# Threshold search of a mixture-of-experts router: one of three counts on ScalarE, mantissa digits in float sums

## The chip, the cores and the metric

The kernel runs on one core of a Trainium2 chip. The metric is the device time of one execution in microseconds. Engines are named as in the profile: PE is TensorE, DVE is VectorE, ACT is ScalarE, POOL is GpSimd, SP issues loads and stores.

## What is computed

One transformer block on x of shape (2, 2048, 256): a modulated layer norm, linear attention with 16 heads, then a second modulated layer norm and a mixture of 8 experts with 2 experts for each token and a capacity of 640 tokens for each expert. The change lies in how the tokens of an expert are picked. Cut to that part, the reference is:

```python
probs = jax.nn.softmax(xf @ router_w.T, axis=-1)          # (4096, 8)
topw, topi = jax.lax.top_k(probs, 2)
topw = topw / (topw.sum(-1, keepdims=True) + 1e-06)
order = jnp.lexsort((-fw, fe))                            # by expert, then by weight, falling
rank = jnp.arange(N * K) - starts[se]
keep = rank < capacity                                    # 640 largest weights of each expert
...
eo = jnp.einsum('ecf,efd->ecd', jax.nn.silu(g) * u, wd)
out = jnp.zeros_like(xf).at[st].add(gathered * (sw * keep)[:, None])
```

So each expert needs the 640 largest of its weights. The kernel does not sort: it finds, for each of the 8 experts at once, the largest threshold that at least 640 weights reach, and takes what lies above it.

## The kernel before, in words

Each engine has a program written out by hand; semaphores order them. There are three stages.

*Attention*, one tile of 128 tokens after the other (32 tiles), as a software pipeline over steps (`step` in each engine's program). POOL's last work in it is, for each tile, `xm` (L479) and `h2` (L483). ACT copies each tile's router logits into `logits` (L603) and signals `lgc`.

*Routing.* `choose` on DVE (L773 to L792) turns logits into the two weights of each token, once for the first 26 tiles and once for the last 6; ACT supplies the exponentials (`exp_logits`, L546). PE transposes the weights (L1292), so that 128 partitions hold 256 weights each, 16 partitions to an expert. Then comes the search: `cand` holds three thresholds as integers whose bits are those of positive floats. The loop over `DIGITS` = 15 base-4 digits, from the top of the exponent down, does one round for each:

- DVE counts in each partition how many weights reach each of the three thresholds (L895, three times, each with a sum as second output in `cnt`),
- PE adds the counts of the partitions of an expert (`same_e`, L1296),
- DVE prepares `base` meanwhile (L899), then compares the three sums with 640 (`beats`, L901), takes the largest digit that passes (`won`, L904) and writes the next three thresholds (`cand`, L906). Each of the three waits for the one before.

The tables `digits` and `swaps` for it are set by POOL at the start, one memset for each element (L442, L443). After the loop the threshold goes to all partitions (L909, PE L1298, L911), masks and counts give each token its slot in the expert, `describe(0)` makes one-hot rows by comparing with `iota_b` (L975), and PE looks up the token numbers with them (L1317). Their result `g_idx` (L989) starts POOL's gathers (L500). `iota_b`, 4096 columns of row numbers, is written by ACT behind the last exponential (L622), and behind it ACT makes the high parts `w_h` of the first six blocks of expert 0's weights (L629), whose low parts DVE makes after the search. `reset` (L494, L496) is set by POOL once all logits are there and is read behind the search.

*Experts.* For each of 8 experts PE runs gate, up and down projections in three passes with high and low parts (L1354, L1368); ACT and DVE work on the hidden values beside it. The expert stage begins once the first gathers have landed.

Of the kernel before, what the change touches and what calls it, by code (L numbers as in the profile page):

```python
# [26 lines left out]
N = B * T  # L27
NT = N // P
# [4 lines left out]
CAP = int(1.25 * N / E)  # L33
# [3 lines left out]
FC = F // P  # L37
# [7 lines left out]
TOP_BIT = 29  # L45
PLACES = ((0, 1), (1, E))
EARLY = NT - 6
DIGITS = (TOP_BIT + 1) // 2
NV = 2
XF = 4  # L50
TILE_BITS = 7
# [71 lines left out]
def build_program(nc, x, w_qkv, w_out, router, wg, wu, wd, c, wmod, rope, consts, out):  # L123
# [10 lines left out]
    with ExitStack() as ctx:  # L134
        def sb(name, shape, dt=F32):
            return ctx.enter_context(nc.sbuf_tensor(name, shape, dt))

        def sem(name):
            return ctx.enter_context(nc.semaphore(name))

        bank = [ctx.enter_context(nc.psum_tensor(f"bank{i}", [P, 512], F32)) for i in range(8)]
# [25 lines left out]
        iota_s = sb("iota_s", [P, P], BF16)  # L167
# [9 lines left out]
        digits = sb("digits", [P, DIGITS, 3], I32)  # L177
        swaps = sb("swaps", [P, DIGITS, 3], I32)
# [60 lines left out]


        big = [sb(f"big{i}", [P, NT, E]) for i in range(8)]
        valT = sb("valT", [P, 2 * P])
        hit = sb("hit", [P, 3, 2 * P], BF16)
# [38 lines left out]
        link_s, plink_s = sem("link_s"), sem("plink_s")  # L282
# [10 lines left out]
        iota_d = sem("iota_d")  # L293
        r_dve, r_act, r_pe = sem("r_dve"), sem("r_act"), sem("r_pe")
        cnt_d, tot_d, wonf_d, won_d, cand_d = (sem(n) for n in ("cnt_d", "tot_d", "wonf_d", "won_d", "cand_d"))
        pre_d = sem("pre_d")
        in_d, tn_d, ri_d = sem("in_d"), sem("tn_d"), sem("ri_d")
        facts_d, look_d, idx_d = (sem(n) for n in ("facts_d", "look_d", "idx_d"))
# [116 lines left out]
        def _(pool):  # L415
# [7 lines left out]
            for i in range(2):  # L423
# [4 lines left out]
                                    pattern=[[1, P]], channel_multiplier=-1).then_inc(plink_s, 1)  # L428
            nc.gpsimd.iota(iota_s[:, :], pattern=[[1, P]], base=0, channel_multiplier=0,
                           allow_small_or_imprecise_dtypes=True).then_inc(plink_s, 1)  # L430
            nc.gpsimd.iota(rev[:, :], pattern=[[-1, E]], base=E, channel_multiplier=0,
                           allow_small_or_imprecise_dtypes=True).then_inc(plink_s, 1)
            nc.gpsimd.iota(tile_id[:, :], pattern=[[1, CT]], base=0, channel_multiplier=0,
                           allow_small_or_imprecise_dtypes=True).then_inc(plink_s, 1)
            nc.gpsimd.iota(vals[:, :, 0], pattern=[[0, NT]], base=0, channel_multiplier=1,
                           allow_small_or_imprecise_dtypes=True).then_inc(plink_s, 1)
            nc.gpsimd.iota(vals[:, :, 1], pattern=[[P, NT]], base=0, channel_multiplier=0,
                           allow_small_or_imprecise_dtypes=True).then_inc(plink_s, 1)
            for n in range(DIGITS):
                unit = 1 << (TOP_BIT - 1 - 2 * n)  # L440
                for d in range(3):
                    nc.gpsimd.memset(digits[:, n, d:d + 1], (d + 1) * unit)  # L442
                    ins = nc.gpsimd.memset(swaps[:, n, d:d + 1], (d + 1) * unit | ((d + 1) * unit >> 2))  # L443
            ins.then_inc(plink_s, 1)

            def step(s):
                on = stages(s)
# [42 lines left out]
            steps(pool, step, ATT)  # L490


            pool.wait_ge(lgc, NT)
            nc.gpsimd.memset(reset[:, :, :], 1.0).then_inc(plink_s, 1)  # L494
            pool.wait_ge(plink_s, 14)
            nc.gpsimd.memset(reset[:, :, 0:1], 0.0).then_inc(plink_s, 1)  # L496
            def gather(e, par):

# [40 lines left out]
        def _(act):  # L539
# [78 lines left out]
            steps(act, step, ATT)  # L618

            exp_logits(EARLY, NT)  # L620
            act.wait_ge(plink_s, 8)
# [12 lines left out]
            def x_high(e, par, g, bk=7):  # L634

# [52 lines left out]
        def _(dve):  # L688
            chain = [0]

            def link(ins):

                chain[0] += 1
                ins.then_inc(link_s, 1)
                dve.wait_ge(link_s, chain[0])

            V = nc.vector
# [61 lines left out]
            TT, RED = V.tensor_tensor, V.tensor_reduce  # L759
# [126 lines left out]

            choose(EARLY, NT)
            for d in range(3):
                ins = V.memset(cand[:, d:d + 1], (d + 1) << (TOP_BIT - 1))
            link(ins)  # L890
            dve.wait_ge(r_pe, 1)
            link(V.tensor_copy(valT[:, :], bank[0][:, 0:2 * P]))
            for n in range(DIGITS):
                for d in range(3):
                    ins = V.tensor_scalar(hit[:, d, :], valT[:, :], cand[:, d:d + 1].bitcast(F32), 0.0, ALU.is_ge,  # L895
                                          ALU.add, accum_out=cnt[:, d:d + 1])
                ins.then_inc(cnt_d, 1)

                TT(base[:, :], cand[:, :], swaps[:, n, :], ALU.bitwise_xor)  # L899
                dve.wait_ge(tot_d, n + 1)  # L900
                V.scalar_tensor_tensor(beats[:, :], bank[1][:, 0:3], float(CAP), digits[:, n, :],  # L901
                                       ALU.is_ge, ALU.mult).then_inc(wonf_d, 1)
# [3 lines left out]
                TT(cand[:, :], base[:, :], won[:, :].to_broadcast([P, 3]), ALU.bitwise_or).then_inc(cand_d, 1)  # L906
                dve.wait_ge(cand_d, n + 1)

            V.tensor_scalar(thr_sel[:, :], sel_e[:, :], cand[:, 0:1].bitcast(F32), None, ALU.mult).then_inc(r_dve, 1)  # L909
            dve.wait_ge(r_pe, 2)  # L910
            link(V.tensor_copy(thr_b[:, :], bank[2][:, 0:E]))  # L911
            dve.wait_ge(plink_s, 15)

            def place_masks(part):

# [236 lines left out]
        def _(pe):  # L1152
            MM = nc.tensor.matmul
# [138 lines left out]
                last = TR(bank[0][:, k * P:(k + 1) * P], flat[:, k * P:(k + 1) * P], ident[:, :])  # L1292
            last.then_inc(r_pe, 1)
            for n in range(DIGITS):
                pe.wait_ge(cnt_d, n + 1)
# [192 lines left out]
```

## Time and profile before

| | us |
|---|---|
| median of 3 runs | 659.88 (659.63 to 659.90) |
| the profiled execution, its own time | 656.8 |
| its span, first to last instruction | 654.9 |
| PE busy | 569.0 (87%) |
| DVE busy | 448.4 (68%) |
| ACT busy | 322.0 (49%) |
| POOL busy | 266.4 (41%) |

The profile tells for one execution when each instruction ran and what it waited for. The busy shares are means over stages that differ: between 228 and 262 us PE was busy for 3.47 us and DVE for 28.39 us. So what an instruction is worth has to be read from the stage in which it stands. The chain of waits follows the end of the kernel back through what released each step; the timeline gives the instructions in order of their starts.

### The profile page before, as it was taken

The page shows a single profiled execution, that of the slowest core. Times are in us where ns is not written, and L with a number is a line of the kernel's source. Part 1 is how long each engine was busy: PE and PEld are TensorE (multiplying, and loading weights), DVE is VectorE, ACT ScalarE, POOL GpSimd, SP SyncE. Part 2 cuts the span into 40 slices and gives each one's busy share as a digit, 9 for nine tenths or more (in the row PEclk, how much of TensorE's full clock was granted, in tenths as well). Part 3 has the DMA queues.
Part 4 walks back from the last instruction along what each step waited for, and adds up shares of the span by engine and source line. Part 5 has one row for each costly group of instructions (what it writes and reads, how often), then busy time and mean ns, then how long its engine had stood idle before and what let it go on. Part 6 is the DMA issues. An engine that isn't in the chain of part 4 may idle for free.

```text
span 654.9 us, 13692 instructions
## 1 busy us (share of the span) xinstructions
PE 569.0 (87%) x4041; PEld 529.9 (81%) x4041; DVE 448.4 (68%) x1250; ACT 322.0 (49%) x717; POOL 266.4 (41%) x428
## 2 busy tenths in 40 slices
PE   4999889999899401399999999999999999999992
PEld 3677678888777300299999999999999999999992
DVE  3577879898677888875756676677567666666441
ACT  3678768887445510044434445445355354454330
POOL 5588747786678400402025043061070250341321
PEclk9999989999899655589999999999999999999997
DMA  5322258744565640232617336347056174260221
GB/s 169 97 66 73 72 155 269 220 145 132 170 188 189 209 105 0 71 108 82 193 51 159 109 89 137 92 104 185 24 118 195 33 155 129 82 137 9 34 25 16
DMA packets 91911, 75.24 MB, mean 115 GB/s; under 512 B 12108, under 2 KB 88278, under 8 KB 91864
## 3 DMA queue, kind: packets, MB, share of 16 engines
q1 hardware_dynamic: 82872, 58.77, 29.7%
q0 software_dynamic: 8992, 15.90, 12.6%
q8 instruction: 24, 0.39, 0.3%
q14 instruction: 23, 0.19, 0.1%
HBM read 52.48 MB, written 22.16 MB: 114 GB/s over the span
## 4 chain that ended last, share of the span: by engine, by line
PE 63%; DVE 12%; issue 4%; POOL 2%; DMA 2%; ACT 2%; SPq 1%; DVEq 0%; ACTq 0%; POOLq 0%
PE bank L1354 29%; PE bank L1368 14%; PE bank L1389 4%; DVE hit L895 3%; PE bank L1272 3%; PE bank L1175 3%; PE bank L1317 3%; PE bank L1403 2%; PE bank L1331 1%; DVE x L864 1%; PE bank L1252 1%; DVE st L866 1%; DMA w_raw<-wd 1%; PE bank L1261 1%; DMA xg<-h_rows,g_idx 1%
## 5 line engine op out<-in xcount | busy, mean ns | idle before, releaser
L500 POOL DMA_INDIRECT xg<-h_rows,g_idx x40 | 40.8, 1019 | 256.5 <-DVE g_idx L989 246.7
L1354 PE MATMUL bank<-xT_h,w_h 128*128 128x320 f32 x448 | 139.4, 311 | 1.2 <-DVE xT_l L1018 1.2
L1354 PE MATMUL bank<-xT_h,w_l 128*128 128x320 f32 x448 | 138.4, 309 | 0.0
L1354 PE MATMUL bank<-xT_l,w_h 128*128 128x320 f32 x448 | 138.4, 309 | 0.0
L656 ACT CAST hid_h<-hid 128x320 fp32r<-128x320 f32 x112 | 51.7, 461 | 82.5 <-DVE hid L1046 82.5
L1046 DVE TENSOR_TENSOR hid<-act_g,bank 128x320 f32<-128x320 f32 x112 | 54.5, 487 | 54.4 <-ACT act_g L652 54.4
L510 POOL DMA_INDIRECT out<-yo,s_idx x40 | 66.3, 1657 | 60.7 <-DVE yo L1036 21.9
L652 ACT ACTIVATE act_g<-bank 128x320 f32<-128x320 f32 x112 | 48.9, 437 | 82.0 <-PE bank L1354 81.4
L1354 PEld LDWEIGHTS bank<-xT_h,w_h 128*128 128x128 f32 x448 | 84.8, 189 | 1.8 <-issue 1.4
L1354 PEld LDWEIGHTS bank<-xT_l,w_h 128*128 128x128 f32 x448 | 84.6, 189 | 0.0
L1354 PEld LDWEIGHTS bank<-xT_h,w_l 128*128 128x128 f32 x448 | 84.5, 189 | 0.0
L1368 PE MATMUL bank<-w_h,hid_h 128*128 128x256 f32 x280 | 80.3, 287 | 0.0
L1051 DVE TENSOR_TENSOR hid_l<-hid,hid_h 128x320 fp32r<-128x320 f32 x112 | 55.0, 491 | 34.1 <-ACT hid_h L656 33.7
L1368 PE MATMUL bank<-w_h,hid_l 128*128 128x256 f32 x280 | 78.3, 280 | 0.0
L1368 PE MATMUL bank<-w_l,hid_h 128*128 128x256 f32 x280 | 78.2, 279 | 0.0
L1004 DVE TENSOR_TENSOR w_l<-w_raw,w_h 128x768 fp32r<-128x768 f32 x64 | 61.1, 960 | 10.1 <-ACT w_h L629 9.7
L1175 PE MATMUL bank<-wqkv_h,hT_h 128*128 128x256 f32 (+1 forms) x128 | 49.8, 389 | 6.0 <-DVE hT_l L836 4.4
L629 ACT CAST w_h<-w_raw 128x768 fp32r<-128x768 f32 x64 | 52.9, 834 | 1.9 <-DMA w_raw<-wd 1.9
L1368 PEld LDWEIGHTS bank<-w_l,hid_h 128*128 128x128 f32 x280 | 53.0, 189 | 0.0
L1368 PEld LDWEIGHTS bank<-w_h,hid_l 128*128 128x128 f32 x280 | 52.8, 189 | 0.0
L1368 PEld LDWEIGHTS bank<-w_h,hid_h 128*128 128x128 f32 x280 | 52.7, 188 | 0.0
L488 POOL TENSOR_TENSOR rot<-rot_a,rot_b 128x512 f32<-128x512 f32 x32 | 42.3, 1321 | 17.9 <-DVE rot_b L829 17.6
(190 smaller groups left out, 1296.0 us busy)
## 6 DMA issues: line engine op xcount, KB each, us to landing
w_raw<-wg SPq DMA_DIRECT2D x32, 256.0 KB, 3.5
w_raw<-wu SPq DMA_DIRECT2D x32, 256.0 KB, 4.6
w_raw<-wd SPq DMA_DIRECT2D x16, 512.0 KB, 5.7
x_in<-x SPq DMA_DIRECT2D x32, 128.0 KB, 2.1
q_store<-qT SPq DMA_DIRECT2D x32, 128.0 KB, 1.9
q_in<-q_store SPq DMA_DIRECT2D x32, 128.0 KB, 2.1
x_re<-x SPq DMA_DIRECT2D x32, 128.0 KB, 2.1
out<-x SPq DMA_DIRECT2D x32, 128.0 KB, 1.9
```

The lines of the kernel that those rows point to most:

```text
L488: nc.gpsimd.tensor_tensor(rot[s.par(0)][:, :], rot_a[:, :], rot_b[:, :], ALU.add).then_inc(rope_d, 1)
L500: nc.gpsimd.indirect_dma_start(out=xg[par][:, a, :], out_offset=None, in_=h2_rows, in_offset=bass.IndirectOffsetOnAxis(ap=g_idx[par][:, a: ...
L510: nc.gpsimd.indirect_dma_start(out=out_rows, out_offset=bass.IndirectOffsetOnAxis(ap=s_idx[par][:, a:a + 1], axis=0), in_=yo[:, a, :], in_ ...
L629: nc.scalar.copy(w_h[:, f, :], w_raw[:, f, :]).then_inc(sp_h, 1)
L652: nc.scalar.activation(act_g[h][:, 0:HCAP], bank[2 * h][:, 0:HCAP], ACT.Silu).then_inc(silu_d, 1)
L656: nc.scalar.copy(hid_h[f % 2][:, h * HCAP:(h + 1) * HCAP], hid[h][:, 0:HCAP]).then_inc(hh_d, 1)
L1004: V.tensor_tensor(w_l[:, f, :], w_raw[:, f, :], w_h[:, f, :].bitcast(F32), ALU.subtract).then_inc(sp_l, 1)
L1046: V.tensor_tensor(hid[h][:, 0:HCAP], act_g[h][:, 0:HCAP], bank[2 * h + 1][:, 0:HCAP], ALU.mult)\
L1051: V.tensor_tensor(hid_l[f % 2][:, h * HCAP:(h + 1) * HCAP], hid[h][:, 0:HCAP], hid_h[f % 2][:, h * HCAP:(h + 1) * HCAP].bitcast(F32), ALU. ...
L1175: ins = MM(out, x[j][:, k, :], w[i][:, k, cols], start=n == 0, stop=n == 3 * KC - 1)
L1354: last = MM(bank[2 * h + m][:, 0:HCAP], W[i][:, f, at:at + P], XT[j][:, k, cols], start=n == 0, stop=n == 3 * KC - 1)
L1368: last = MM(bank[4 + a // 2][:, a % 2 * D:(a % 2 + 1) * D], (hid_h, hid_l)[j][f % 2][:, a * P:(a + 1) * P], (w_h, w_l)[i][:, f, 4 * P:], s ...
```

## The change

Five things are changed.

1. ACT counts the smallest of the three thresholds, with a Sign and a summed output; DVE counts the other two. A sum of signs is not a count, so a matmul of `offset` and `ones_r` puts 640 in the first column of the sums beforehand, and DVE now counts weights *below* a threshold. The weights are stored shifted left by one with the lowest bit set (`valT`), so that no weight equals a threshold.
2. The first 4 digits (the exponent) are found as before. The last 11 (the mantissa) are found with float sums: `pieces` holds the steps of every digit, the comparison sums itself into `wins`, and `cand` is made from `wins` in one instruction. `won` falls away there.
3. `iota_b` is written by POOL, behind its last attention work and ahead of its wait for the logits.
4. ACT's six casts of `w_h` stand between its counts, in rounds 1 to 6.
5. The tables that POOL sets at the start are smaller.

```diff
+HEAD_DIGITS = 4
+OVER_ONE = 0x7F400000
+TAIL_DIGITS = DIGITS - HEAD_DIGITS
+FEWER = float(N - CAP)
...
# POOL, at the start
-            for n in range(DIGITS):
-                unit = 1 << (TOP_BIT - 1 - 2 * n)
+            for n in range(HEAD_DIGITS):
+                unit = 1 << (TOP_BIT - 2 * n)
+                follow = unit >> 2 if n < HEAD_DIGITS - 1 else 0
...
+            for n in range(TAIL_DIGITS):
+                for d in range(3):
+                    nc.gpsimd.memset(parts[:, n, d:d + 1], (d + 1) * 4.0 ** -(n + 1))
+            nc.gpsimd.memset(offset[:, :], 0.0)
+            nc.gpsimd.memset(ones_r[:, :], 1.0).then_inc(plink_s, 1)
...
# POOL, behind the attention steps
+            nc.gpsimd.iota(iota_b[:, :, :], pattern=[[1, P], [0, NT]], base=0, channel_multiplier=0,
+                           allow_small_or_imprecise_dtypes=True).then_inc(iota_d, 1)
             pool.wait_ge(lgc, NT)
...
# ACT
-            nc.scalar.copy(iota_b[:, :, :], iota_s[:, :].unsqueeze(2).to_broadcast([P, P, NT])).then_inc(iota_d, 1)
-            for f in range(FC - 2):
-                split_high(0, f, f)
+            act.wait_ge(val_d, 1)
+            for n in range(DIGITS):
+                act.wait_ge(cand_d, n + 1)
+                    nc.scalar.activation(side[:, :], valT[:, :].bitcast(F32), ACT.Sign, bias=cand[:, 0:1].bitcast(F32),
+                                         scale=-1.0, accum_out=cnt[:, 0:1]).then_inc(side_d, 1)
+                if 1 <= n < FC - 1:
+                    split_high(0, n - 1, n - 1)
...
# DVE
-            link(V.tensor_copy(valT[:, :], bank[0][:, 0:2 * P]))
+            V.tensor_scalar(valT[:, :], bank[0][:, 0:2 * P].bitcast(I32), 1, 1, ALU.logical_shift_left, ALU.bitwise_or)\
+                .then_inc(val_d, 1)
...
+            def count_below(n):
+                for d in range(1, 3):
+                    ins = V.tensor_scalar(hit[:, d - 1, :], valT[:, :].bitcast(F32), cand[:, d:d + 1].bitcast(F32), 0.0, ALU.is_lt,
                                           ALU.add, accum_out=cnt[:, d:d + 1])
                 ins.then_inc(cnt_d, 1)
...
+                if n == HEAD_DIGITS - 2:
+                    link(ins)
+                    ins = V.tensor_scalar(cand[:, 2:3], cand[:, 2:3], OVER_ONE, None, ALU.min)
...
+            link(TT(pieces[:, :, :].rearrange("p n d -> p (n d)"), parts[:, :, :].rearrange("p n d -> p (n d)"),
+                    lead_f[:, 0:1].to_broadcast([P, TAIL_DIGITS * 3]), ALU.mult))
+            TT(cand_f, lead_f[:, 0:1].to_broadcast([P, 3]), pieces[:, 0, :], ALU.add).then_inc(cand_d, 1)
+            for n in range(HEAD_DIGITS, DIGITS):
+                t = n - HEAD_DIGITS
+                count_below(n)
+                V.scalar_tensor_tensor(base_f, pieces[:, t, :], -0.75 if n < DIGITS - 1 else -1.0, cand_f, ALU.mult, ALU.add)
+                dve.wait_ge(tot_d, n + 1)
+                V.tensor_scalar(beats[:, :], bank[1][:, 0:3], FEWER, 0.0, ALU.is_le, ALU.add, accum_out=wins[:, :])\
+                    .then_inc(won_d, 1)
+                dve.wait_ge(won_d, n + 1)
+                V.scalar_tensor_tensor(cand_f, pieces[:, t, 0:1].to_broadcast([P, 3]), wins[:, :], base_f, ALU.mult, ALU.add)\
+                    .then_inc(cand_d, 1)
+                dve.wait_ge(cand_d, n + 2)
+            link(V.tensor_scalar(won[:, :], cand[:, 0:1], 1, None, ALU.logical_shift_right))
...
# PE
             for n in range(DIGITS):
+                if n:
+                    pe.wait_ge(won_d, n)
+                MM(bank[1][:, 0:3], ones_r[:, :], offset[:, :], start=True, stop=False)
                 pe.wait_ge(cnt_d, n + 1)
-                MM(bank[1][:, 0:3], same_e[:, :], cnt[:, :], start=True, stop=True).then_inc(tot_d, 1)
+                pe.wait_ge(side_d, n + 1)
+                MM(bank[1][:, 0:3], same_e[:, :], cnt[:, :], start=False, stop=True).then_inc(tot_d, 1)
```

The change moves instructions at two places on which much depends. The first is ACT behind the last exponential (`big<-big` is that exponential, `side,cnt` the Sign with its sum). Before:

```order
L546 ACTIVATE big<-big 128x48 [waits r_act]
L622 COPY iota_b<-iota_s 128x4096 [waits plink_s]
L629 CAST w_h<-w_raw 128x768 [waits raw_a] x4
L629 CAST w_h<-w_raw 128x768 [waits raw_b] x2
L638 CAST xT_h<-bank 128x2x256 [waits trx_d]
```

Now:

```order
L566 ACTIVATE big<-big 128x48 [waits r_act]
L653 ACTIVATE side,cnt<-valT,cand 128x256 [waits cand_d,val_d]
L653 ACTIVATE side,cnt<-valT,cand 128x256 [waits cand_d]
L647 CAST w_h<-w_raw 128x768 [waits raw_a]
L653 ACTIVATE side,cnt<-valT,cand 128x256 [waits cand_d]
```

The copy is gone, and a cast now follows each of the counts of rounds 1 to 6; after the last of them eight counts stand alone.

The second is POOL at the end of its attention work. Before:

```order
L479 TENSOR_TENSOR xm<-xn_1,mod_all 128x256 [waits h2_d,norm2]
L483 TENSOR_TENSOR h_1<-xm,mod_all 128x256 [waits tr_h2,st_h21,pm2]
L494 MEMSET reset 128x512 [waits lgc]
L496 MEMSET reset 128x16 [waits plink_s]
```

Now:

```order
L497 TENSOR_TENSOR xm<-xn_1,mod_all 128x256 [waits h2_d,norm2]
L501 TENSOR_TENSOR h_1<-xm,mod_all 128x256 [waits tr_h2,st_h21,pm2]
L511 IOTA iota_b 128x4096
L514 MEMSET reset 128x512 [waits lgc]
L516 MEMSET reset 128x16 [waits plink_s]
```

The iota has no wait of its own, so it runs right behind `h_1`, ahead of the wait for the logits.

## Rows read from the trace of the kernel before

**Rows 1.** The page's head.
```profile
span 654.9 us, 13692 instructions
```

**Rows 2.** Chain of waits, first round of the search: start us, us, what.
```profile
228.10 1.30 DVE hit L895 x6
...
229.45 0.20 PE bank L1296
229.68 0.17 DVE beats L901
...
230.26 1.30 DVE hit L895 x6
...
260.21 0.17 DVE cand L906
```

**Rows 3.** Timeline, counts of the first round: start us, us, engine, line, operation.
```profile
228.51 0.48 DVE L895 TENSOR_SCALAR_CACHE_REDUCE hit<-valT,cand 128x256 bf16<-128x256 f32 x1
...
229.31 0.09 DVE L895 DVE_READ_ACCUMULATOR hit<-valT,cand 128x1 bf16 x1
```

**Rows 4.** Waits, 215 to 285 us: total us, times, longest us.
```profile
POOL xg L500 <- DVE g_idx L989: 45.4, 1, 45.4
```

**Rows 5.** Groups by line and shape on ACT: busy us, mean ns, idle before.
```profile
L608 ACT ACTIVATE xn<-x,sh,rs 128x256 f32<-128x256 f32 x32 | 19.3, 604 | 13.5 <-POOL sh L471 13.4
...
L677 ACT ACTIVATE act_g<-bank 128x256 f32<-128x256 f32 x8 | 3.1, 384 | 5.4 <-PE bank L1389 5.3
L603 ACT COPY logits<-bank 128x8 f32<-128x8 f32 x18 | 3.0, 167 | 9.5 <-PE bank L1261 9.2
```

**Rows 6.** Timeline, ACT ahead of and in the search.
```profile
223.76 3.59 ACT L622 COPY iota_b<-iota_s 128x4096 bf16<-128x4096 bf16 x1
...
227.26 4.49 ACT L629 CAST w_h<-w_raw 128x768 fp32r<-128x768 f32 x6
```

**Rows 7.** Small DVE instructions: timeline of L909; by line L785, L783 (ns min/median/max).
```profile
260.40 0.23 DVE L909 TENSOR_SCALAR thr_sel<-const_sb,cand 128x8 f32<-128x8 f32 x1
...
L785 DVE TENSOR_SCALAR small<-small x2: 170/175/180, 220.7 to 225.4; 128x26 f32<-128x26 f32 x1, 128x6 f32<-128x6 f32 x1
...
L783 DVE SCALAR_TENSOR_TENSOR small<-small x2: 166/177/188, 220.2 to 225.0; 128x26 f32<-128x26 f32 x1, 128x6 f32<-128x6 f32 x1
```

**Rows 8.** Timeline, POOL's iotas at the start.
```profile
3.62 0.24 POOL L429 IOTA iota_s<- 128x128 bf16 x1
3.83 0.13 POOL L431 IOTA rev<- 128x8 f32 x1
...
4.00 0.17 POOL L435 IOTA vals<- 128x32 bf16 x1
4.11 0.16 POOL L437 IOTA vals<- 128x32 bf16 x1
```

**Rows 9.** Timeline, end of POOL's attention work beside `choose` on DVE.
```profile
216.82 0.72 POOL L479 TENSOR_TENSOR xm<-xn,mod_all 128x256 f32<-128x256 f32 x1
216.85 0.92 DVE L776 TENSOR_TENSOR big<-big,rev 128x208 f32<-128x208 f32 x1
...
218.21 0.38 DVE L778 TENSOR_TENSOR big<-big,small 128x208 f32<-128x208 f32 x1
...
219.31 0.73 POOL L483 TENSOR_TENSOR h<-xm,mod_all 128x256 f32<-128x256 f32 x1
220.68 0.18 DVE L785 TENSOR_SCALAR small<-small 128x26 f32<-128x26 f32 x1
...
223.15 0.19 DVE L773 TENSOR_REDUCE small<-logits 128x6 f32<-128x48 f32 x1
```

**Rows 10.** Timeline, POOL and DVE in an early attention step.
```profile
18.71 1.46 POOL L488 TENSOR_TENSOR rot<-rot_a,rot_b 128x512 f32<-128x512 f32 x1 [3.07 <-DVE rot_b L829]
18.94 0.15 DVE L746 TENSOR_SCALAR nm<-mv 128x1 f32<-128x1 f32 x1
```

**Rows 11.** Timeline, PE at the start.
```profile
7.36 3.55 PE L1166 MATMUL bank<-cT,wmod_sb 128*128 128x2 f32 x16 [2.83 <-DMA wmod_sb<-wmod]
```

More of the change, by code:

```diff
@@ L176, in build_program @@
         won, beats = sb("won", [P, 1], I32), sb("beats", [P, 3])
-        digits = sb("digits", [P, DIGITS, 3], I32)
-        swaps = sb("swaps", [P, DIGITS, 3], I32)
+        wins, lead = sb("wins", [P, 1]), sb("lead", [P, 3], I32)
+        digits = sb("digits", [P, HEAD_DIGITS, 3], I32)
+        swaps = sb("swaps", [P, HEAD_DIGITS, 3], I32)
+        parts = sb("parts", [P, TAIL_DIGITS, 3])
+        pieces = sb("pieces", [P, TAIL_DIGITS, 3])
+        offset = sb("offset", [1, 3], BF16)
+        ones_r = sb("ones_r", [1, P], BF16)
         cnt = sb("cnt", [P, 3], BF16)
@@ L241, in build_program @@
         big = [sb(f"big{i}", [P, NT, E]) for i in range(8)]
-        valT = sb("valT", [P, 2 * P])
-        hit = sb("hit", [P, 3, 2 * P], BF16)
+        valT = sb("valT", [P, 2 * P], I32)
+        hit = sb("hit", [P, 2, 2 * P], BF16)
+        side = sb("side", [P, 2 * P], BF16)
         reset = sb("reset", [P, 2 * E, NT])
@@ L295, in build_program @@
         cnt_d, tot_d, wonf_d, won_d, cand_d = (sem(n) for n in ("cnt_d", "tot_d", "wonf_d", "won_d", "cand_d"))
+        side_d, val_d = sem("side_d"), sem("val_d")
         pre_d = sem("pre_d")
@@ L438, in _ @@
                            allow_small_or_imprecise_dtypes=True).then_inc(plink_s, 1)
-            for n in range(DIGITS):
-                unit = 1 << (TOP_BIT - 1 - 2 * n)
+            for n in range(HEAD_DIGITS):
+                unit = 1 << (TOP_BIT - 2 * n)
+                follow = unit >> 2 if n < HEAD_DIGITS - 1 else 0
                 for d in range(3):
                     nc.gpsimd.memset(digits[:, n, d:d + 1], (d + 1) * unit)
-                    ins = nc.gpsimd.memset(swaps[:, n, d:d + 1], (d + 1) * unit | ((d + 1) * unit >> 2))
-            ins.then_inc(plink_s, 1)
+                    nc.gpsimd.memset(swaps[:, n, d:d + 1], (d + 1) * (unit | follow))
+            for n in range(TAIL_DIGITS):
[3 more added lines that the diff above has]
+            nc.gpsimd.memset(ones_r[:, :], 1.0).then_inc(plink_s, 1)
+            pool.wait_ge(plink_s, 13)
+            nc.gpsimd.memset(offset[:, 0:1], float(CAP)).then_inc(plink_s, 1)
             def step(s):
@@ L490, in _ @@
             steps(pool, step, ATT)
+            nc.gpsimd.iota(iota_b[:, :, :], pattern=[[1, P], [0, NT]], base=0, channel_multiplier=0,
+                           allow_small_or_imprecise_dtypes=True).then_inc(iota_d, 1)
             pool.wait_ge(lgc, NT)
             nc.gpsimd.memset(reset[:, :, :], 1.0).then_inc(plink_s, 1)
-            pool.wait_ge(plink_s, 14)
+            pool.wait_ge(plink_s, 15)
             nc.gpsimd.memset(reset[:, :, 0:1], 0.0).then_inc(plink_s, 1)
@@ L620, in _ @@
             exp_logits(EARLY, NT)
-            act.wait_ge(plink_s, 8)
-            nc.scalar.copy(iota_b[:, :, :], iota_s[:, :].unsqueeze(2).to_broadcast([P, P, NT])).then_inc(iota_d, 1)
             def split_high(e, f, count, implied=False):
@@ L629, in split_high @@
                 nc.scalar.copy(w_h[:, f, :], w_raw[:, f, :]).then_inc(sp_h, 1)
-            for f in range(FC - 2):
-                split_high(0, f, f)
+            act.wait_ge(val_d, 1)
+            for n in range(DIGITS):
+                act.wait_ge(cand_d, n + 1)
+                with nc.allow_low_precision(reason="sums of 256 signs are whole and exact"):
+                    nc.scalar.activation(side[:, :], valT[:, :].bitcast(F32), ACT.Sign, bias=cand[:, 0:1].bitcast(F32),
+                                         scale=-1.0, accum_out=cnt[:, 0:1]).then_inc(side_d, 1)
+                if 1 <= n < FC - 1:
+                    split_high(0, n - 1, n - 1)
             def x_high(e, par, g, bk=7):
@@ L888, in _ @@
             for d in range(3):
-                ins = V.memset(cand[:, d:d + 1], (d + 1) << (TOP_BIT - 1))
+                ins = V.memset(cand[:, d:d + 1], (d + 1) << TOP_BIT)
             link(ins)
+            dve.wait_ge(plink_s, 14)
             dve.wait_ge(r_pe, 1)
-            link(V.tensor_copy(valT[:, :], bank[0][:, 0:2 * P]))
-            for n in range(DIGITS):
-                for d in range(3):
-                    ins = V.tensor_scalar(hit[:, d, :], valT[:, :], cand[:, d:d + 1].bitcast(F32), 0.0, ALU.is_ge,
+            V.tensor_scalar(valT[:, :], bank[0][:, 0:2 * P].bitcast(I32), 1, 1, ALU.logical_shift_left, ALU.bitwise_or)\
+                .then_inc(val_d, 1)
+            dve.wait_ge(val_d, 1)
+            dve.sem_inc(cand_d, 1)
+            def count_below(n):
+                for d in range(1, 3):
+                    ins = V.tensor_scalar(hit[:, d - 1, :], valT[:, :].bitcast(F32), cand[:, d:d + 1].bitcast(F32), 0.0, ALU.is_lt,
                                           ALU.add, accum_out=cnt[:, d:d + 1])
                 ins.then_inc(cnt_d, 1)
+            for n in range(HEAD_DIGITS):
+                count_below(n)
                 TT(base[:, :], cand[:, :], swaps[:, n, :], ALU.bitwise_xor)
                 dve.wait_ge(tot_d, n + 1)
-                V.scalar_tensor_tensor(beats[:, :], bank[1][:, 0:3], float(CAP), digits[:, n, :],
-                                       ALU.is_ge, ALU.mult).then_inc(wonf_d, 1)
+                V.scalar_tensor_tensor(beats[:, :], bank[1][:, 0:3], FEWER, digits[:, n, :],
+                                       ALU.is_le, ALU.mult).then_inc(wonf_d, 1)
                 dve.wait_ge(wonf_d, n + 1)
@@ L905, in _ @@
                 dve.wait_ge(won_d, n + 1)
-                TT(cand[:, :], base[:, :], won[:, :].to_broadcast([P, 3]), ALU.bitwise_or).then_inc(cand_d, 1)
-                dve.wait_ge(cand_d, n + 1)
-            V.tensor_scalar(thr_sel[:, :], sel_e[:, :], cand[:, 0:1].bitcast(F32), None, ALU.mult).then_inc(r_dve, 1)
+                ins = TT((cand if n < HEAD_DIGITS - 1 else lead)[:, :], base[:, :], won[:, :].to_broadcast([P, 3]), ALU.bitwise_or)
+                if n == HEAD_DIGITS - 2:
+                    link(ins)
+                    ins = V.tensor_scalar(cand[:, 2:3], cand[:, 2:3], OVER_ONE, None, ALU.min)
+                if n < HEAD_DIGITS - 1:
+                    ins.then_inc(cand_d, 1)
+                    dve.wait_ge(cand_d, n + 2)
+            link(ins)
+            cand_f, base_f, lead_f = (t[:, :].bitcast(F32) for t in (cand, base, lead))
+            link(TT(pieces[:, :, :].rearrange("p n d -> p (n d)"), parts[:, :, :].rearrange("p n d -> p (n d)"),
+                    lead_f[:, 0:1].to_broadcast([P, TAIL_DIGITS * 3]), ALU.mult))
+            TT(cand_f, lead_f[:, 0:1].to_broadcast([P, 3]), pieces[:, 0, :], ALU.add).then_inc(cand_d, 1)
+            dve.wait_ge(cand_d, HEAD_DIGITS + 1)
+            for n in range(HEAD_DIGITS, DIGITS):
+                t = n - HEAD_DIGITS
+                count_below(n)
+                V.scalar_tensor_tensor(base_f, pieces[:, t, :], -0.75 if n < DIGITS - 1 else -1.0, cand_f, ALU.mult, ALU.add)
[5 more added lines that the diff above has]
+                    .then_inc(cand_d, 1)
+                dve.wait_ge(cand_d, n + 2)
+            link(V.tensor_scalar(won[:, :], cand[:, 0:1], 1, None, ALU.logical_shift_right))
+            V.tensor_scalar(thr_sel[:, :], sel_e[:, :], won[:, :].bitcast(F32), None, ALU.mult).then_inc(r_dve, 1)
             dve.wait_ge(r_pe, 2)
             link(V.tensor_copy(thr_b[:, :], bank[2][:, 0:E]))
-            dve.wait_ge(plink_s, 15)
+            dve.wait_ge(plink_s, 16)
             def place_masks(part):
@@ L1294, in _ @@
             for n in range(DIGITS):
+                if n:
+                    pe.wait_ge(won_d, n)
+                else:
+                    pe.wait_ge(plink_s, 14)
+                MM(bank[1][:, 0:3], ones_r[:, :], offset[:, :], start=True, stop=False)
                 pe.wait_ge(cnt_d, n + 1)
-                MM(bank[1][:, 0:3], same_e[:, :], cnt[:, :], start=True, stop=True).then_inc(tot_d, 1)
+                pe.wait_ge(side_d, n + 1)
+                MM(bank[1][:, 0:3], same_e[:, :], cnt[:, :], start=False, stop=True).then_inc(tot_d, 1)
             pe.wait_ge(r_dve, 3)
```

## The prediction

> **What bounds the kernel now.** I read the page first for the span [rows 1], then the chain of waits around the threshold search, since the change touches little else. From 228.10 to 260.40 us the chain holds nothing but the search: fifteen identical rounds, one for each base-4 digit. One round is 2.15 us: 1.30 us in which VectorE counts against three thresholds, a 0.20 us matmul on TensorE that sums the counts, and then `beats`, `won` and `cand`, each waiting for the one before, from 229.68 to the next count at 230.26, so 0.58 us for three and 0.19 us for each [rows 2]. 15 rounds fill (260.40 - 228.10) = 32.3 us, 4.9% of the span of 654.9 us [rows 1, 2, 7].
>
> The timeline tells what the 1.30 us are made of: counts start every 0.40 us, each is drained only after 0.48 us, and the readout of the last sum ends at 229.40 [rows 3]. So three counts are 3 x 0.405 + 0.085. VectorE, not TensorE, sets the pace; TensorE and ScalarE have nothing urgent. What hangs on the end of the search is seen in the waits: the first gather on POOL sat 45.4 us until VectorE had `g_idx` [rows 4], and its indices come out of the threshold. No load is late there: the longest wait of that issue is for VectorE. So a microsecond less in the search should be a microsecond less in the kernel, and a microsecond more in front of it, in `choose`, a microsecond more.
>
> **The change part by part.**
>
> (a) One threshold leaves VectorE: 15 x 0.405 = 6.1 us less [rows 2, 3].
>
> (b) ScalarE counts it with a Sign. Its price is not in the trace, so it is bounded. Below: an activation of 256 columns with constants, 0.38 us. Above: one of 256 columns with two per-partition operands, 0.60 us. The Sign has one such operand, so I take the middle, 0.49 us [rows 5]. The readout of its sum is at least free and at most about one more tiny instruction, 0.17 us [rows 5]; I take the upper end. With 0.03 us from `cand` to its start it is ready after 0.69 us (at most 0.80). VectorE's two counts take 2 x 0.405 + 0.085 + 0.03 = 0.93 us. So ScalarE's count is hidden by 0.24 us (at least 0.13) and costs nothing; without that cover every 0.1 us is 1.5 us in 15 rounds.
>
> (c) The six casts of `w_h` now stand between ScalarE's counts in rounds 1 to 6, each behind the count of its round. Six in a row took 4.49 us, so one holds the engine for 0.73 us [rows 6]. Count and cast end by 0.69 + 0.73 = 1.42 us after `cand`, and the next count is asked for after 1.63 us or more (the new round, below). Cost 0; the cover is 0.2 us, and the next count has its own 0.24 us behind that.
>
> (d) In the last 11 rounds `won` goes: `beats` sums its own comparisons, and `cand` multiplies by that sum. Ideally 0.19 us each, 2.1 us in all. But two things are added: the readout of a sum, which ends some 0.02 us after the main instruction [rows 3], and a per-partition operand. L909 with such an operand takes 0.23 us for 8 columns, L785 with constants 0.17 us for 6, so 0.06 us [rows 7]. The saving is 0.19 - 0.02 - 0.06 = 0.11, with rounding 0.12 us, in 11 rounds 1.3 us. Bounds: 2.1 us, or nothing if the readout costs its whole 0.09 us and the operand more.
>
> (e) Once only: the cap on `cand` (0.18), `pieces` (0.22), the first float `cand` (0.19) and the shift back at the end (0.19), all chained and priced as the small instructions of rows 2 and 7 with 33 columns for `pieces`: 0.8 us more. The shift in `valT` takes the place of a copy out of the same bank: 0.
>
> (f) TensorE's extra matmul of `offset` waits for `won_d`, 0.2 to 0.4 us before `cand`, and then has the whole next count, 0.93 us, to run its 0.2 us. Queued behind it is only the matmul of the same round. Cost 0, if the wait for two engines in place of one costs no more than 0.05 us (0.75 us in all, kept for the range).
>
> Rounds are then 2.15 - 0.40 = 1.75 us (four) and 1.63 us (eleven). (a) to (f) give 6.1 + 1.3 - 0.8 = 6.6 us less.
>
> (g) `iota_b` moves from ScalarE, where it took 3.59 us [rows 6] beside VectorE's `choose` and cost nothing, to POOL, which starts it as soon as its last `h` is done, 219.31 + 0.73 = 220.04 us [rows 9], since it stands ahead of POOL's wait for the logits. Price on POOL: the spacing of 128 columns is 0.21 us, of 32 columns 0.11 us, so 1.04 ns for a column [rows 8]; 4096 of them are 4.3 us, to 224.4 us. The `reset` memsets behind it are wanted only after the search. The other end is the price of POOL's arithmetic, 0.73 us for 256 columns, 2.85 ns for each [rows 9].
>
> Does it disturb VectorE? The trace has a clear case that POOL can: L776 began 0.03 us after POOL's L479 and took 0.92 us, where L778 of the same width took 0.38; it ended 0.23 us after POOL was through [rows 9]. Both read two tiles. On the other side L746, one column, ran in 0.15 us in the middle of a long POOL instruction [rows 10]. An iota reads nothing, and no row has VectorE beside one as long. The instruction at risk is L785: one tile read, one written, and 20 columns more cost it 10 ns where they cost L783 22 ns [rows 7], so it moves two columns at a time and seems to need twice the access. It starts at 220.68, inside the iota. If it is held to 224.4 + 0.2, it ends at 224.6 in place of 220.86, and everything behind it in `choose` moves by 3.75 us; VectorE goes from one half of `choose` into the other without a gap (at 223.15 [rows 9]), so nothing absorbs it. Between 0 and 3.75 us I take 3.75, by the nearest row, L776.
>
> The Trainium skill (SBUF — State Buffer, Who interferes with whom) states that VectorE and GpSimd share a pair of ports as an exclusive lock, that an instruction with two inputs contends only with a GpSimd instruction that reads, but that one in a two-port mode, which `tensor_scalar` can enter, contends with GpSimd. The trace agrees for L776; for L785 beside an iota no run shows it yet. Applied to L785 it gives the sum with the hold; applied to the two-input instructions alone it gives the sum without.
>
> (h) POOL sets 30 fewer constants at the start. TensorE waits there for `wmod` until 7.36 us and then works 3.55 us [rows 11] before it takes POOL's first result. Worth 0; an x load that starts earlier may help or hurt by 0.3 us.
>
> **Sum**: -6.6 + 3.75 = -2.85 us. The profiled execution, 656.8 us with its span of 654.9, would go to about 654.0. The median of the three runs, 659.88, lies 3.1 us above it; I keep that distance, so the forecast is 657.0 us.
>
> **Rivals.**
> 1. *No hold.* The iota only writes, and L785 passes as L746 did. All 6.6 us are kept: 653.3 us, with the ideal tail of (d) 652.5 us. For it: rows 10, and that VectorE's two-input instructions are not met by a POOL instruction that reads. Against it: L785's slope.
> 2. *ScalarE's count becomes the last one.* If Sign and readout are ready 1.23 us after `cand` in place of 0.69, each round loses 0.3 us, 4.5 us in all: 657.8 us without the hold, 661.5 with it. It decides from 0.93 us after `cand`. Against it: no ScalarE row of this width is over 0.60 us.
> 3. *Slower: a dear iota that holds VectorE.* Place: L785 at 220.68. If the iota costs 2.85 ns a column, it runs 11.7 us to 231.7, VectorE loses 11.0 us, and the kernel takes 659.88 - 6.6 + 11.0 = 664.3 us. It turns slower than before from an iota of 7.2 us (1.8 ns a column). Against it: the iotas and memsets of POOL are near 1 ns.
> 4. *The tail is not shorter.* The readout and the operand eat the 0.12 us, the wait for two engines 0.05 us: 2 us less gain, 659.0 with the hold.
>
> **How the numbers follow.** Chances: the forecast with the hold 0.50 (it contains rival 4 at its upper end), no hold 0.32, rival 2 0.09, rival 3 0.05, something unseen 0.04. A measurement of this kernel can tell about 0.2%, 1.3 us, from no change. Faster by more than that means under 658.56: nearly all of the forecast's case (0.45), all of no hold (0.32), most of rival 2 (0.06): 0.83. Slower: rival 3 and part of rival 2 and of the unseen, 0.07. Same: the rest, 0.10. The range reaches from no hold with the ideal tail, 652.4, to the hold with rival 4, 659.0. The likeliest case's own range is 656.0 to 659.0.
>
> **What would show it.** In the changed profile: `hit` 30 times, starts 0.40 us apart; rounds of 1.75 and 1.63 us, from the starts of `cand`; the matmul released by VectorE and not by ScalarE; no gap in ScalarE's order of count and cast. The iota at 220 us with 4.3 us, and L785's successor with several us in place of 0.18. If that instruction takes 0.18 us, (g) was wrong and rival 1 right. If the matmul waits for `side`, (b) was wrong. If the stretch behind the search, from the threshold to the first gather, is not as long as before, the claim that all of the search lies on the path is wrong.

## The result and the profile after

The changed kernel takes 653.34 us (median of 13 runs) against 659.63 us before (13 runs): ratio 0.9913, 95% interval 0.9897 to 0.9929, which is 5.7 us less (4.7 to 6.8); the two medians by themselves differ by 6.3. The profiled execution took 653.2 us, its span is 651.4 us, against 656.8 and 654.9 us before, so 3.5 us of span less. Two later measurements of the same kernel gave 0.9940 (0.9917 to 0.9962) and 0.9926 (0.9900 to 0.9952).

The timeline at the end of POOL's attention work, beside `choose` on VectorE; it answers to [rows 9]:

```profile
215.72 0.72 POOL L497 TENSOR_TENSOR xm<-xn,mod_all 128x256 f32<-128x256 f32 x1
215.75 0.92 DVE L800 TENSOR_TENSOR big<-big,rev 128x208 f32<-128x208 f32 x1
...
218.90 4.17 POOL L511 IOTA iota_b<- 128x4096 bf16 x1
219.08 0.18 DVE L807 SCALAR_TENSOR_TENSOR small<-small 128x26 f32<-128x26 f32 x1
...
219.58 3.53 DVE L809 TENSOR_SCALAR small<-small 128x26 f32<-128x26 f32 x1
...
219.67 3.44 DVE L810 TENSOR_TENSOR big<-big,rev 128x208 f32<-128x208 f32 x1
...
223.15 0.32 DVE L811 RECIPROCAL small<-small 128x26 f32<-128x26 f32 x1
...
225.12 0.19 DVE L797 TENSOR_REDUCE small<-logits 128x6 f32<-128x48 f32 x1
```

L809 is the L785 of before, same instruction, same width: 3.53 us in place of 0.18, from 219.58 to 223.11, 0.04 us behind the end of the iota (223.07). L807, with two inputs, ran in its usual 0.18 us while the iota was under way. Only L809 is held; L810 stands in the queue behind it.

The start of the search and one round of its last eleven, in the timeline; it answers to [rows 3]:

```profile
229.65 0.42 DVE L917 TENSOR_SCALAR valT<-bank 128x256 int32<-128x256 int32 x1 [0.86 <-PE bank L1347]
230.23 0.51 ACT L653 ACTIVATE side<-valT,cand 128x256 bf16<-128x256 f32 x1 [4.39 <-DVEq L920]
230.26 0.48 DVE L925 TENSOR_SCALAR_CACHE_REDUCE hit<-valT,cand 128x256 bf16<-128x256 f32 x1 [0.18 <-DVE valT L917]
...
244.42 0.51 ACT L653 ACTIVATE side<-valT,cand 128x256 bf16<-128x256 f32 x1 [1.03 <-DVE cand L959]
244.42 0.48 DVE L925 TENSOR_SCALAR_CACHE_REDUCE hit<-valT,cand 128x256 bf16<-128x256 f32 x1
...
244.83 0.47 DVE L925 TENSOR_SCALAR_CACHE_REDUCE hit<-valT,cand 128x256 bf16<-128x256 f32 x1
244.84 0.19 ACT L653 ACTIVATION_READ_ACCUMULATOR side<-valT,cand 128x1 bf16 x1
245.23 0.09 DVE L925 DVE_READ_ACCUMULATOR hit<-valT,cand 128x1 bf16 x1
...
245.37 0.19 PE L1357 MATMUL bank<-cnt,same_e 128*128 128x3 bf16 x1 [1.00 <-DVE hit L925]
245.60 0.16 DVE L956 TENSOR_SCALAR_CACHE_REDUCE beats<-bank 128x3 f32<-128x3 f32 x1 [0.21 <-PE bank L1357]
245.68 0.08 DVE L956 DVE_READ_ACCUMULATOR beats<-bank 128x1 f32 x1
245.80 0.22 DVE L959 SCALAR_TENSOR_TENSOR cand<-pieces,wins,base 128x3 f32<-128x3 f32 x1
...
246.06 0.51 ACT L653 ACTIVATE side<-valT,cand 128x256 bf16<-128x256 f32 x1 [1.03 <-DVE cand L959]
```

The round is 246.06 - 244.42 = 1.64 us. ScalarE's sum is read out at 245.03, VectorE's at 245.32: TensorE is released by VectorE, and ScalarE's count has 0.29 us of cover. The waits from 215 to 285 us, which answer to [rows 2, 4], say the same for all 15 rounds:

```profile
POOL xg L520 <- DVE g_idx L1044: 41.1, 1, 41.1
...
PE bank L1357 <- DVE hit L925: 15.9, 15, 1.6
```

From the timelines of both kernels the stretch that the change touches can be cut into four parts by the starts of its instructions. It explains 3.3 us:

| part | before | after | difference |
|---|---|---|---|
| `choose`, first half (first to second `small<-logits`) | 7.40 | 10.47 | +3.07 |
| second half, transposes, `valT` (to the first count) | 4.95 | 5.14 | +0.19 |
| search (first count to `thr_sel`) | 32.30 | 25.79 | -6.51 |
| `thr_sel` to `g_idx` | 7.66 | 7.62 | -0.04 |

### The profile page after: what moved, and what is told of

It is laid out like the page before. It is cut to its first block, busy times and chain, and to the rows that moved or that the text cites. A ratio compares the mean times of both kernels' runs of the same rounds, so it can differ in the third digit from the quotient of the medians.

```text
span 651.4 us, 13713 instructions
## 1 busy us (share of the span) xinstructions
PE 569.6 (87%) x4056; PEld 530.2 (81%) x4056; DVE 445.2 (68%) x1224; ACT 327.0 (50%) x746; POOL 269.4 (41%) x399
## 4 chain that ended last, share of the span: by engine, by line
PE 63%; DVE 11%; issue 4%; POOL 3%; DMA 3%; ACT 1%; SPq 1%; DVEq 0%; POOLq 0%; ACTq 0%
PE bank L1415 31%; PE bank L1429 15%; PE bank L1450 4%; PE bank L1378 3%; PE bank L1327 2%; DVE hit L925 2%; PE bank L1464 2%; PE bank L1392 1%; PE bank L1230 1%; DVE x L888 1%; DMA mod_all<-mod_store 1%; DVE st L890 1%; DMA x_in<-x 1%; PE bank L1307 1%; PE bank L1316 1%
```

## The experiments

The table has each kernel's measured ratio beside what the parts say. "Parts" is the sum of the four parts of its own profile less the 52.31 us of the kernel before, also as a ratio to that kernel's time in the same job.

A job runs several kernels and the kernel before on one chip, and the chips differ: the kernel before took 657.5 us beside the late iota, the two inputs, the 30 memsets and the changed kernel's second measurement, 666.9 us beside the iota alone, the three counts, the integers and the two Signs, and 658.6 us beside the unchanged kernel, the iota twice and the changed kernel's third measurement. So times compare only within a job. Profiles of the same kernel agree within 0.1 us in the sum of the parts.

| kernel | first half | search | parts, us | parts, ratio | measured ratio (95%) |
|---|---|---|---|---|---|
| changed, first | 10.47 | 25.79 | -3.3 | 0.9950 | 0.9913 (0.9897 to 0.9929) |
| changed, second | 10.48 | 25.80 | -3.3 | 0.9950 | 0.9940 (0.9917 to 0.9962) |
| changed, third | 10.47 | 25.79 | -3.3 | 0.9951 | 0.9926 (0.9900 to 0.9952) |
| late iota | 7.40 | 25.80 | -6.3 | 0.9904 | 0.9887 (0.9859 to 0.9916) |
| two inputs | 7.41 | 25.79 | -6.3 | 0.9904 | 0.9904 (0.9878 to 0.9929) |
| 30 memsets more | 10.47 | 25.78 | -3.3 | 0.9951 | 0.9923 (0.9895 to 0.9952) |
| iota alone, on before | 10.47 | 32.30 | +3.0 | 1.0046 | 1.0051 (1.0031 to 1.0070) |
| three counts on VectorE | 10.48 | 31.79 | +2.8 | 1.0041 | 1.0014 (0.9990 to 1.0038) |
| all digits in integers | 10.47 | 26.70 | -2.4 | 0.9964 | 0.9934 (0.9905 to 0.9962) |
| two Signs | 10.47 | 28.41 | -0.6 | 0.9990 | 0.9970 (0.9949 to 0.9990) |
| before, unchanged | 7.39 | 32.33 | 0.0 | 1.0000 | 1.0003 (0.9983 to 1.0023) |
| iota twice | 10.47 | 25.78 | -3.2 | 0.9952 | 0.9909 (0.9880 to 0.9937) |

### The iota later

```diff
-            nc.gpsimd.iota(iota_b[:, :, :], ...).then_inc(iota_d, 1)
             pool.wait_ge(lgc, NT)
...
+            pool.wait_ge(r_dve, 2)
+            nc.gpsimd.iota(iota_b[:, :, :], ...).then_inc(iota_d, 1)
```

> The changed kernel, but POOL writes iota_b only after choose is done (it waits for the second wgt), beside the search, whose VectorE instructions are not of the held kind. Hold theory: L809 falls from 3.53 us to 0.18 us, choose from 10.47 to 7.4 us (start of the first small to start of the second), the kernel is 3.1 us faster than the changed one, ratio to before about 0.987. Rival (the 3.53 us are taken elsewhere or would be absorbed behind): no change against the changed kernel, ratio 0.991 or more.

Timeline of POOL and of VectorE:

```profile
219.24 0.18 DVE L810 TENSOR_SCALAR small<-small 128x26 f32<-128x26 f32 x1
```
```profile
225.44 4.18 POOL L516 IOTA iota_b<- 128x4096 bf16 x1 [3.06 <-DVE wgt L817]
```

The former L809 (here L810) is back at 0.18 us, `choose` at 7.40, and the search beside the iota is as long as ever, 25.80. 649.82 us against 653.65 for the changed kernel in the same job. The hold is what the early iota costs: 3.07 us by the parts, 3.8 us by the medians of these two kernels.

### Which instruction is held

```diff
-                V.tensor_scalar(den, den, 1.0, None, ALU.add)
+                V.scalar_tensor_tensor(den, den, 1.0, den, ALU.add, ALU.max)
```

> The changed kernel with the iota where it is, but the one-tile instruction L809 (den + 1) is written as an instruction with two inputs from SBUF and the same result. If the hold strikes only one-input instructions that move two columns at a time, L809 runs in about 0.18 us beside the iota and the kernel is 3.1 us faster than the changed one, ratio 0.987. If a POOL iota holds every VectorE instruction that uses a second port, it is held as before: L809 about 3.5 us, ratio as the changed kernel, 0.991 to 0.995.

Timeline, the iota in its early place:

```profile
220.90 4.18 POOL L511 IOTA iota_b<- 128x4096 bf16 x1
...
221.58 0.19 DVE L809 SCALAR_TENSOR_TENSOR small<-small 128x26 f32<-128x26 f32 x1
221.69 0.37 DVE L810 TENSOR_TENSOR big<-big,rev 128x208 f32<-128x208 f32 x1
222.09 0.32 DVE L811 RECIPROCAL small<-small 128x26 f32<-128x26 f32 x1
222.32 0.31 DVE L812 TENSOR_REDUCE small<-big 128x26 f32<-128x208 f32 x1
```

The maximum of den + 1 and den is den + 1, so the result is the same. Written with two inputs, the sum on the same tile passes the iota in 0.19 us, and every instruction behind it too, the reciprocal and the reductions with their single input included. So an iota, which only writes, holds this `tensor_scalar` with one input, the one that by its slope of 0.5 ns a column moves two columns at a time, and no other instruction that ran beside it in `choose`. The kernel was 2.4 us faster than the changed one in the same job, but the two ratios' intervals overlap (0.9878 to 0.9929 and 0.9917 to 0.9962); what decides is the trace. The Trainium skill (SBUF — State Buffer, Who interferes with whom) has both halves: two inputs contend only with a GpSimd instruction that reads, a two-port mode contends with GpSimd. The traces here agree with both, by 0.19 and 3.53 us.

### The iota alone, on the kernel before

```diff
-            nc.scalar.copy(iota_b[:, :, :], iota_s[:, :].unsqueeze(2).to_broadcast([P, P, NT])).then_inc(iota_d, 1)
...
+            nc.gpsimd.iota(iota_b[:, :, :], ...).then_inc(iota_d, 1)
             pool.wait_ge(lgc, NT)
```

> The kernel before with one part of the change alone: iota_b on POOL, ahead of its wait for the logits, in place of ScalarE's copy. Hold theory: the one-tile instruction of choose (L783 to L787) takes some 3.5 us, choose 10.47 us in place of 7.40, the search stays at 32.3 us; 3.1 us slower than before, ratio about 1.005. Rival (the hold needs ScalarE's idleness or another part of the change): ratio 1.000.

```profile
221.22 4.17 POOL L493 IOTA iota_b<- 128x4096 bf16 x1
```
```profile
221.90 3.53 DVE L785 TENSOR_SCALAR small<-small 128x26 f32<-128x26 f32 x1
```

Measured 1.0051 (1.0031 to 1.0070): this part by itself makes the kernel slower.

### The iota twice

An iota of the same size into an unused tile stands ahead of the one for `iota_b`.

> The changed kernel with a second iota of 4096 columns ahead of the first, into a tile that nobody reads. If the port passes only when POOL has nothing queued, L809 takes 7.7 us, choose 14.7 us, and the kernel is 4.2 us slower than the changed one, ratio about 1.001, so slower than without the change by as much as rival 3 said for an iota of 8.4 us. If the waiting VectorE instruction gets in between the two, L809 still takes about 3.5 us and the ratio is that of the changed kernel.

```profile
219.25 4.17 POOL L512 IOTA iota_c<- 128x4096 bf16 x1
...
219.93 3.53 DVE L812 TENSOR_SCALAR small<-small 128x26 f32<-128x26 f32 x1
...
223.39 4.17 POOL L514 IOTA iota_b<- 128x4096 bf16 x1
...
227.50 0.52 POOL L517 MEMSET reset<- 128x512 f32 x1
...
227.69 0.36 DVE L812 TENSOR_SCALAR small<-small 128x6 f32<-128x6 f32 x1
```

L812 is the L809 of the changed kernel. The hold lasts for one POOL instruction, not for what is queued: L812 ended at 223.46 while the second iota was running. The kernel was not slower than the changed one. The last two rows show a memset doing the same on a small scale: the narrow L812 took 0.36 us in place of 0.17 and ended with `reset`.

### The start of POOL's program

Thirty memsets of one column more in front of the attention steps.

> The changed kernel with 30 more memsets of one column on POOL at the start, so that its start is as long as before. By the prediction's step on the tables this is worth 0 (within 0.3 us): ratio as the changed kernel. Rival: the measured gain over the one seen in the profile (5.7 against 3.5 us) comes from the shorter start; then this kernel is about 2 us slower than the changed one.

653.02 us against 653.65 in the same job. POOL's first attention instruction (`rs`) started at 7.42 us in this kernel, at 6.43 in the changed one and at 7.20 in the kernel before, so the start was indeed as long as before. The 2 us of the rival do not show, and step (h), worth 0, stands within the intervals.

### Three counts on VectorE

The Sign is gone, `count_below` runs over `range(3)`, and the offset is zero.

> The changed kernel with the first threshold counted by VectorE again (three counts), no Sign on ScalarE, the offset matmul of zeros left in. Step (a): each of the 15 rounds 0.40 us longer, search 25.8 + 6.1 = 31.9 us, 6.1 us slower than the changed kernel, ratio about 1.003. Rival (the third count is not what bounds a round): less than 3 us.

Search 31.79 us, so 6.00 us more for 15 counts, 0.40 each: step (a). The ratio lies below what the parts say; more on that at the end.

### All digits in integers

`HEAD_DIGITS = DIGITS`, the loop of the tail and `pieces` left out.

> The changed kernel with all 15 digits found as the first four are, in integers with three chained instructions; the one-time float steps (pieces, first cand) fall away. Steps (d) and (e): 11 rounds of 1.75 in place of 1.63 us, +1.3 us, less 0.4 us for the one-time steps: search about 26.7 us in place of 25.8. Rival (the tail brings nothing): search 25.4 us.

Search 26.70 us, 0.91 more than with the float tail. Timeline of one round:

```profile
245.37 0.16 DVE L933 SCALAR_TENSOR_TENSOR beats<-bank,digits 128x3 f32<-128x3 f32 x1 [0.21 <-PE bank L1340]
245.56 0.16 DVE L936 TENSOR_REDUCE won<-beats 128x1 int32<-128x3 f32 x1
245.75 0.16 DVE L938 TENSOR_TENSOR cand<-base,won 128x3 int32<-128x3 int32 x1
...
245.95 0.51 ACT L653 ACTIVATE side<-valT,cand 128x256 bf16<-128x256 f32 x1 [1.15 <-DVE cand L938]
```

From `beats` to the next count it is 0.58 us, with the sum in one operation 0.46 (245.60 to 246.06 above): 0.12 us for each of 11 rounds. The chained operation saved is worth less than the 0.19 us that it took.

### Two Signs

> The changed kernel with a second Sign on ScalarE in each round, without a sum, ahead of the counting one. It adds about 0.42 us on ScalarE, of which step (b) says that 0.24 us or so are covered by VectorE's two counts: rounds without a cast become 0.1 to 0.25 us longer and the matmul is released by ScalarE in place of VectorE; search 27.3 to 29.5 us. If ScalarE already bounded a round, the rounds would be 0.42 us longer and the search 32.1 us; if its cover were larger than 0.42 us, nothing would change.

The waits of TensorE, and a round in the timeline:

```profile
PE bank L1360 <- ACT side L656: 17.7, 14, 1.7
```
```profile
243.59 0.09 DVE L928 DVE_READ_ACCUMULATOR hit<-valT,cand 128x1 bf16 x1
...
243.60 0.19 ACT L656 ACTIVATION_READ_ACCUMULATOR side<-valT,cand 128x1 bf16 x1
...
243.93 0.16 PE L1360 MATMUL bank<-cnt,same_e 128*128 128x3 bf16 x1 [1.57 <-ACT side L656]
```

Now ScalarE releases TensorE, in 14 of 15 rounds. The search is 28.41 us, 0.17 us a round more. The added Sign delays ScalarE's sum by 0.41 us (242.79 to 243.20), so 0.24 us were covered, as step (b) had it. By the readouts alone it was 0.29 us; but here TensorE starts 0.14 us behind ScalarE's readout (243.79 to 243.93), where it starts 0.05 us behind VectorE's (245.32 to 245.37 above).

### The controls

> The changed kernel once more, as the mark for the others of this chip. Account by the trace: search -6.5 us, valT +0.2, choose +3.1, together -3.2 us, ratio 0.995. If the ratio is again near 0.991, some 2.5 us of the gain lie outside the stretch from choose to the first gather, and its windows against the kernel before should show where.

> The kernel before, unchanged, as a control of the measurement: ratio 1.000 within the interval. Its profile gives a second sample of how long the attention stage (start to the first small of choose) and the expert stage (g_idx to the end) last without the change. If the change gains outside its own stretch, these are longer here than in the changed kernel's profile of the same chip; if the extra gain of the first measurement was spread of the runs, they agree.

> The changed kernel a third time. From the account of the stretch (choose +3.1, valT +0.2, search -6.5) the ratio is 0.995; a gain outside the stretch of about 2.5 us would make it 0.991.

The measurement finds no difference where there is none (1.0003). What differs between executions lies outside the stretch. In the same job, the span of the unchanged kernel was 659.8 us and that of the changed one (third measurement) 652.3. Of these 7.5 us, the stretch gives 3.3, and the stage behind `g_idx` 3.7 (391.4 against 387.7 us). One cause is visible at the end of expert 0, in the waits of TensorE from 278 us on, first the unchanged, then the changed kernel:

```profile
PE bank L1317 <- DVE xT_l L1018: 2.1, 1, 2.1
```
```profile
PE bank L1378 <- DVE xT_l L1073: 1.2, 1, 1.2
```

Over all profiles this wait is between 0.6 and 2.1 us, on either side of the change (1.4 and 2.1 in the two profiles of the kernel before, 0.6, 1.8 and 1.2 in the three of the changed one). Behind it TensorE does only the small matmuls of the lookup, and in most profiles the granted clock then falls from 1.0 to 0.5 (1.2 in place of 2.4 GHz) for some microseconds. Windows of 2 us: their length, the busy time of PE, PEld, DVE, ACT and POOL, then the clock, DMA share and GB/s. First the unchanged kernel in its second profile, where it fell, then the same kernel in its first, where it did not, then the changed kernel in its first:

```profile
326.00:328.00 2.00, 0.01 (x1) 0.01 (x1) 1.44 (x4) 1.68 (x3) 0.00 (x0) 1.00 0.06 19
328.00:330.00 2.00, 2.00 (x32) 2.00 (x33) 0.94 (x1) 0.00 (x0) 0.00 (x0) 0.80 0.00 0
330.00:332.00 2.00, 2.00 (x10) 2.00 (x10) 0.00 (x0) 0.00 (x0) 0.00 (x0) 0.50 0.00 0
```
```profile
328.00:330.00 2.00, 2.00 (x18) 2.00 (x17) 0.00 (x0) 0.00 (x0) 0.00 (x0) 1.00 0.00 0
```
```profile
324.00:326.00 2.00, 2.00 (x10) 2.00 (x9) 0.00 (x0) 0.00 (x0) 0.00 (x0) 0.50 0.00 0
```

The length of this wait alone does not tell whether the clock falls: it stayed at 1.00 after 1.4 us in the first profile of before, and fell in all three profiles of the changed kernel, after 0.6, 1.8 and 1.2 us. So nothing shows that this fall favours the changed kernel, but it makes executions of one kernel differ.

Multiply, for each window of the stage behind `g_idx`, its length by 1 less the granted clock, and add up: the unchanged kernel's two profiles give 10.8 and 16.5 us, and the stage took 386.8 and 391.4 us. The sums differ by 5.7 us and the stages by 4.6, so the clock is enough to explain why these two executions differ. In the changed kernel's three profiles the sums are 14.7, 13.5 and 14.7 us and the stage took 387.7, 388.7 and 387.7 us.

## Why the prediction was right, and where not

The median, 653.34 us, lies in the range, and the sign was right. The size was not: the forecast's case gave 2.85 us less, measured were 5.7 (4.7 to 6.8). The likeliest case's own range, 656.0 to 659.0, was missed. The time lies in the whole range only because that made room for rival 1, "no hold", which named 653.3 us and whose mechanism did not occur; that the number fits is luck. (The lower end, 652.4, is 0.1 below the prediction's own sum, 652.5.) Point by point:

- **(a)** 6.1 us predicted, 6.0 measured. Right.
- **(b)** Sign 0.49 predicted, 0.51 measured; readout 0.17 predicted, 0.19 measured, of which 0.09 us lie under the Sign (244.84 to 244.93), so the sum is there 0.61 us after the start. Cover 0.24 predicted, 0.24 by the doubled Sign. Rival 2 did not occur.
- **(c)** Right. In the rounds of the tail that follow a cast, ScalarE has been idle for 0.31 us when `cand` comes (timeline).
- **(d)** 0.12 us a round, 1.3 us, as measured. Rival 4 did not occur: the wait for two engines costs nothing that shows.
- **(e)** 0.8 us predicted. The search as a whole went from 32.30 to 25.79 us, 6.51 less where (a) to (f) gave 6.6, so this sum was right to 0.1. But the shift into `valT` was put at 0, and the first count starts 0.61 us after it (229.65 to 230.26) where it was 0.45 (227.65 to 228.10), so 0.16 us later. A wait for `valT` stood there before too; new between is a signal to ScalarE (L920). That it costs the 0.16 us was not tested.
- **(f), (h)** Right within what can be seen.
- **(g)** The hold is shown, by three runs in which it goes or comes with the iota or with the form of one instruction. Its size, 3.75 us, was 3.07. Three terms were off: the iota took 4.17 us and not 4.3; the held instruction ended 0.04 us behind it and not 0.2; and L810 ended together with L809, so that L811 began 0.04 us behind L809's end and not 0.31 as before (221.17 against 220.86). The argument was right in one half only. L785's slope pointed to what happened; L776, which the prediction called the nearest row, did not: like L807 and L808 it has two inputs, and those passed the iota unheld. Rival 3's price was not near: a column costs 1.02 ns.

The parts thus give -3.3 us, ratio 0.9950, and this lies 2 thousandths outside the interval of the first measurement (to 0.9929), inside that of the second and at the very edge of the third (to 0.9952). The step that failed is "I keep that distance", 3.1 us between the profiled execution and the median. In the changed kernel the two agree within 0.2 us (653.2 and 653.34), and the unchanged kernel's other profile lay 2.9 us above its median (661.75 and 658.85): the distance is spread of the executions, in good part that of the clock.

Every kernel with the new search came out at or below its parts, by 0 to 4 thousandths; the iota alone and the unchanged kernel did not. Two to three thousandths are 1 to 2 us. The 30 memsets speak against the shorter start. An earlier `g_idx` does not explain it either: with three counts on VectorE `g_idx` comes 2.8 us later than before and the ratio is still 0.0027 below the parts, with two inputs it comes 6.3 us earlier and nothing is left over. Less the sums of the clock given above, the stage behind `g_idx` takes 376.0 and 374.9 us in the two profiles before and 373.0, 375.3 and 373.1 us after, so if the remainder is real it may lie there; five profiles that differ by 2 us among themselves do not show it. A shift of the tiles' addresses by the new, smaller tables was not tried. Since the attention stage took 214.4 to 219.0 us in three profiles of one job in which its program is the same (all digits in integers, two Signs, three counts), and the stage behind `g_idx` differed by 4.6 us between two profiles of one kernel, it stays open whether this remainder is one of the change's effects or spread.

Faster than before by more than the change are the two kernels that keep the search and avoid the hold: 0.9887 (0.9859 to 0.9916) with the iota later and 0.9904 (0.9878 to 0.9929) with the two-input form, against 0.9940 (0.9917 to 0.9962) for the changed kernel in the same job. For the two-input form the intervals overlap.

## What to carry to other kernels

Work that costs nothing on an idle engine can hold up another one: before moving a long POOL instruction beside VectorE, look for VectorE instructions with one input whose time grows by half a nanosecond a column, and either delay the move or write those with two inputs. In a round of chained small operations, count each at its full spacing (0.19 us here) but give back what the merged form adds: a readout and a per-partition operand left 0.12. And where a second engine takes a share of a count, its cover can be measured by doubling its work.

## What had not been expected of the hardware

- One VectorE instruction of 0.18 us took 3.35 us more beside an iota that reads nothing; the hold ends between two POOL instructions even when the next one is queued (L812 ended at 223.46, the second iota started at 223.39). A memset of 0.52 us holds in the same way.
- ScalarE's readout of a sum takes 0.19 us but delays the next instruction by only 0.09 us: a cast started at 240.03 where the readout had started at 239.94.
- The granted clock fell to 0.50 in the middle of the expert stage, behind a wait of 2.1 us and 32 small matmuls, in one of two profiles of the same unchanged kernel, and stayed at 1.00 in the other, after a wait of 1.4 us; in the changed kernel it fell after a wait of only 0.6 us.
